# A graph and FFN kernel on one Trainium2 core: a ring of six one-tile one-hot units, one-hots made four (DVE) and five (ACT) slots ahead, and POOL's subtraction set behind the fold of position 35

## The chip, the cores and the metric

The kernel runs on one core of a Trainium2 chip. The metric is device time in microseconds (us) of one execution. The core has a matrix engine (PE, whose weight loads the profile lists as PEld), a vector engine (DVE), a scalar or activation engine (ACT), a general engine (POOL, also called GpSimd) and a queue for transfers (SP). Each runs its own instruction list strictly in order, and they meet at semaphores.

## The reference, cut to what matters

There are 8 batches of 1024 nodes with 128 channels. A graph layer takes for every node the elementwise maximum of its first 25 neighbours' normalised features, and an FFN with routed experts follows.

```python
x = x + gnn(adj, layernorm(x), W, b)
x = x + ffn(layernorm(x), route_id, Wi, bi, Wr, br, Ws, bs, Wo, bo)

def gnn(A, X, W, b):
    mask = A != 0
    scores = where(mask, -arange(N), -inf)
    vals, idx = top_k(scores, 25)
    feats = where(valid[..., None], X[idx], -inf)
    agg = feats.max(axis=2)
    agg = where(degree <= 25, maximum(agg, 0), agg)
    return relu(concat([X, agg]) @ W + b)
```

## The kernel before, in words

**The neighbour maximum as matmuls.** Nodes lie in eight tiles of 128. The first tile (the hub tile, with many neighbours) goes by a top-25 search on DVE and a gather of rows: POOL issues 25 indirect transfers a batch (`gather`, L508), the first 13 as one half and the last 12 as the other, two at a time (PACE is 2: the next pair waits until the last has landed). The other seven tiles of columns go through PE. For each source tile (or pair of tiles, group 5) and each rank r within it, the r-th neighbour of every node is picked by a one-hot matrix: PE multiplies the features of the source tile by it. Such a pair (group, rank) is a **slot**; there are NS = 44 slots to a batch, in the order of PLACES. Position p is the place of a slot in this order, and n = 44 * batch + p its number. A slot of full width has 7 tiles (896 columns, as 512 + 384); a narrow one has fewer. Positions 1, 13, 19, 20, 24 and 42 belong to the two-tile group 5 and have twice the matmuls and a one-hot of two tiles.

**The three steps of a slot.** (1) The one-hot is made in SBUF from `rank`: on DVE by one comparison (`tensor_scalar`, is_equal, L926) for the 16 positions of DVE_HOT (3, 5, 7, 13, 15, 16, 18, 19, 20, 23, 24, 31, 33, 36, 38, 42), on ACT for the 28 of ACT_HOT, by one activation (L636) where r is 1, otherwise by a square into `away` (`distance`, L625) and a second activation (L642). (2) PE runs the slot (`slot`, L730) into one of two PSUM buffers: it waits for the one-hot and for the fold of slot n - 2, which frees the buffer. (3) DVE folds the result into the running maximum `acc` (`fold_slot`, L937 for positions 0 and 1, L939 for the others), after PE has ended the slot.

**The ring before.** `onehot` has RING = 3 places of two tiles. ACT waits for slot n - 3 before it writes one-hot n. DVE needs no wait, as it writes one-hot n right behind its fold of slot n - 3 (AHEAD = 3).

**The order of the work.** All engines walk over (s, p), s from 0 to 9, p from 0 to 43. In stage s, batch s is prepared (masks, transposes, ranks, top-25), the slots of batch s - 1 are run, and the FFN of batch s - 2 (`finish`) is computed. So stages 1 to 8 hold slots, stage 9 holds only an FFN. What else is done at which position is written out by hand in tables. Those that matter here:

- ACT: at p = 7 the square root for the norms (L658), which waits for DVE's variance of the same position; at 9 and 11 four activations `h` each (L567); at 11, 13, 14, 16 the normalised `xn`; layer activations (L584) at 19 to 34; the ranks' evictions (L596) at 16, 18, 20, 22, 28, 32, 37, 38. ACT runs its one-hot for p + 3 and its square for p + 4 at the end of position p.
- DVE: variance at 7 and reciprocal root at 8 (small operations with drains between them); the search (`score`, `top`, L990, L998, L1000) at 11, 13, 17, 20, 21, 22, 25, 27; the gathered rows' maximum at 14 and 24 (first half) and 31 and 34 (second half). DVE's one-hot for p + 3 follows the fold of p.
- POOL: `split(b)` (L496) computes the low part of the features of batch b, `xsplit[:, b % 2, 1] = xn - xsplit[:, b % 2, 0]`, 1024 columns of float32. PE's slot 0 of the batch waits for it. Before, it is issued after the last gather of batch b - 1, in stage b.

Of the kernel before, what the change touches and what calls it, by code (L numbers as in the profile page):

```python
# [8 lines left out]
F32R = mybir.dt.float32r  # L9
# [6 lines left out]
P = 128  # L16
# [6 lines left out]
SPLITS = 3  # L23
PARTS = 2
CHUNKS = 2
AHEAD = 3
RING = 3
MASKS = 3
HALF = 13
PACE = 2  # L30
# [21 lines left out]
NS = len(SLOTS)  # L52
# [5 lines left out]
AWAYS = 2  # L58


def gnn_ffn_program(nc, x, adj, gnn_W, gnn_b, route_id, Wi, bi, Wr, br, Ws, bs, Wo, bo, out):
# [4 lines left out]
    COLS = TT * P  # L66
# [41 lines left out]
    W_AT = {14: [(0, 0)], 15: [(0, 1)], 16: [(1, 0)], 17: [(1, 1)]}  # L108
    LAYER_AT = [{19 + i: i for i in range(IT)}, {27 + i: i for i in range(IT)}]
    VERDICT_AT = 24  # L110
    FIRST_W_AT = 6
    OUT_AT = {36: 0, 39: 1}
    WEIGHTS_AT = [] + [NS + p for p in (
# [15 lines left out]
    with ExitStack() as ctx:  # L129
        def sb(name, shape, dt=F32):  # L130
            return ctx.enter_context(nc.sbuf_tensor(name, shape, dt))
# [41 lines left out]
        mask = sb("mask", [P, MASKS, N], BF16)  # L173
        at = sb("at", [P, IT, COLS], BF16)
        rank = sb("rank", [P, 2, IT, COLS], BF16)
        onehot = sb("onehot", [P, RING, 2, COLS], F32R)
        away = sb("away", [P, AWAYS, COLS], BF16)
        acc = sb("acc", [P, 2, COLS])
        aggT = sb("aggT", [P, COLS])
# [130 lines left out]
        def positions():  # L310

            for s in range(B + 2):
                for p in range(NS):
                    yield s, p

        def norms(s):

# [147 lines left out]
        @block.gpsimd  # L465
        def _(pool):
            pool.memset(ident[:, :], 0.0).then_inc(s_memset, 1)
            pool.memset(onesb[:, :], 1.0).then_inc(s_memset, 1)
            pool.wait_ge(s_memset, 2)
            pool.affine_select(out=ident[:, :], in_=ident[:, :], compare_op=ALU.not_equal, fill=1.0,  # L470
                               base=0, pattern=[[-1, P]], channel_multiplier=1).then_inc(s_memset, 1)

            pool.affine_select(out=before[:, :], in_=onesb[:, :], compare_op=ALU.is_gt, fill=0.0,
                               base=0, pattern=[[1, P]], channel_multiplier=-1).then_inc(s_memset, 1)
            pool.wait_ge(s_memset, 4)
            pool.affine_select(out=before[:, :], in_=before[:, :], compare_op=ALU.not_equal, fill=-float(NONE - 1),
                               base=0, pattern=[[1, P]], channel_multiplier=-1).then_inc(s_const, 1)
            pool.tensor_copy(identr[:, :], ident[:, :]).then_inc(s_const, 1)
            pool.iota(down[:, :], [[-1, N]], N, channel_multiplier=0,
                      allow_small_or_imprecise_dtypes=True).then_inc(s_const, 1)  # L480
            pool.iota(ranks[:, :], [[1, 32]], 1, channel_multiplier=0,
                      allow_small_or_imprecise_dtypes=True).then_inc(s_const, 1)
            pool.iota(base[:, :], [[1, 1]], N, channel_multiplier=0,
                      allow_small_or_imprecise_dtypes=True).then_inc(s_const, 1)
            pool.iota(lane[:, :], [[1, 1]], 0, channel_multiplier=1,
                      allow_small_or_imprecise_dtypes=True).then_inc(s_const, 1)
            pool.memset(gath[:, HALF:HALF + B, :], 0.0).then_inc(s_const, 1)
            pool.wait_ge(s_const, CONSTS)
            for q in range(4):
                pool.wait_ge(s_adj[q], 16)  # L490
            for b in range(B):
                pool.dma_start(tables[b][N:TABROW, :], gath[:, HALF + b, :]).then_inc(s_zero, 16)
            def split(b):

                pool.wait_ge(s_hi, b + 1)
                pool.tensor_tensor(xsplit[:, b % 2, 1], xn[:, :, :], xsplit[:, b % 2, 0].bitcast(F32),  # L496
                                   ALU.subtract).then_inc(s_split, 1)

            def gather(b, h, entries, signal, reduced):

                pool.wait_ge(s_idx, b * HUBS + h + 1)
                if b + h > 0:
                    pool.wait_ge(reduced, b * HUBS + h)
                pool.wait_ge(s_tab[b % 2], 16 * (b // 2 + 1))
                for i, j in enumerate(entries):
                    if i > 0 and i % PACE == 0:
                        pool.wait_ge(signal, 16 * (len(entries) * (b * HUBS + h) + i))
                    pool.indirect_dma_start(gath[:, j, :], None, tables[b],  # L508
                                            bass.IndirectOffsetOnAxis(ap=idx[:, b % 2, h, j:j + 1], axis=0)
                                            ).then_inc(signal, 16)  # L510

            split(0)
            for m in range(NIN):
                pool.dma_start(w_in[m], raw_weight(m)).then_inc(s_wfirst[m // 4], 16)
            for n, (g, t, cap) in enumerate(CAP_RUNS):
                if t == 0:
                    pool.memset(caps[:, g:g + 1], float(cap)).then_inc(s_caps, 1)
                else:
                    pool.wait_ge(s_caps, n)
                    pool.affine_select(out=caps[:, g:g + 1], in_=caps[:, g:g + 1], compare_op=ALU.is_gt,  # L520
                                       fill=float(cap), base=t * B, pattern=[[-1, 1]], channel_multiplier=-1
                                       ).then_inc(s_caps, 1)
            pool.wait_ge(s_zero, 16 * B)
            for b in range(B):
                for h in range(HUBS):
                    gather(b, h, range(HALF), s_gathA, s_redA)
                    gather(b, h, range(HALF, TOPK), s_gathB, s_redB)
                if b + 1 < B:
                    split(b + 1)

            def tile_again(t, b, one, dma):
                pool.wait_ge(s_const, CONSTS)
                pool.wait_ge(r_idx, one)
                for j in range(TOPK):
                    pool.indirect_dma_start(gath[:, j, :], None, tables[b],
                                            bass.IndirectOffsetOnAxis(ap=idx[:, 0, 0, j:j + 1], axis=0)
                                            ).then_inc(r_gath, 16)
            again(pool, tile_again)

        @block.scalar  # L540
        def _(act):
# [86 lines left out]
            def one_hot(n):  # L628
                b, p = divmod(n, NS)
                g, r, wide = SLOTS[p]  # L630
                first, many = GROUPS[g]
                if n >= RING:
                    act.wait_ge(s_slot, n - RING + 1)
                if r == 1:
                    act.wait_ge(s_q, 2 * IT * b + 2 * (first + many))
                    act.activation(onehot[:, n % RING, 0:many, 0:wide * P],  # L636
                                   rank[:, b % 2, first:first + many, 0:wide * P],
                                   ACT.Relu, bias=ranks[:, 1:2], scale=-1.0).then_inc(s_acthot, 1)
                else:
                    i = b * len(SQUARED) + SQUARED.index(p)  # L640
                    act.wait_ge(s_away, i + 1)
                    act.activation(onehot[:, n % RING, 0, 0:wide * P], away[:, i % AWAYS, 0:wide * P],  # L642
                                   ACT.Relu, bias=1.0, scale=-1.0).then_inc(s_acthot, 1)

            for s, p in positions():
# [17 lines left out]
                if s < B and p in MASK_AT[s > 0]:  # L663
# [3 lines left out]
                    if n >= MASKS:  # L667
                        act.wait_ge(s_turn[n % MASKS], 16 * (n // MASKS))
                    act.activation(mask[:, n % MASKS, :], adj_sb[:, q % 4, :].bitcast(U32), ACT.Sign  # L669
                                   ).then_inc(s_mask, 1)  # L670
                for ahead, body, slots in ((AHEAD, one_hot, ACT_HOT), (AHEAD + 1, distance, SQUARED)):
                    n = (s - 1) * NS + p + ahead
                    if 0 <= n < B * NS and n % NS in slots:
                        body(n)
# [32 lines left out]
        def _(pe):  # L707
# [6 lines left out]
            def slot(b, p):  # L714
# [11 lines left out]
                for j in range(many):  # L726
                    for part in range(PARTS):
                        for c0 in range(0, wide * P, BANK):
                            c1 = min(c0 + BANK, wide * P)
                            mm = pe.matmul(slot_ps[n % 2][:, c0:c1], xsplit[:, b % 2, part, first + j, :],  # L730
                                           onehot[:, n % RING, j, c0:c1], start=(j == 0 and part == 0),
                                           stop=(j == many - 1 and part == PARTS - 1))
                mm.then_inc(s_slot, 1)

# [171 lines left out]
        def _(dve):  # L906
# [13 lines left out]
            def one_hot(n):  # L920
# [2 lines left out]
                first, many = GROUPS[g]  # L923
                if p == min(q for q in DVE_HOT if SLOTS[q][0] == g):
                    dve.wait_ge(s_q, 2 * IT * b + 2 * (first + many))
                dve.tensor_scalar(onehot[:, n % RING, 0:many, 0:wide * P],  # L926
                                  rank[:, b % 2, first:first + many, 0:wide * P], ranks[:, r - 1:r], None,
                                  ALU.is_equal).then_inc(s_onehot, 1)

# [221 lines left out]
            for s, p in positions():  # L1151
                if 1 <= s <= B:
                    fold_slot(s - 1, p)
                ahead = (s - 1) * NS + p + AHEAD
                if 0 <= ahead < B * NS and ahead % NS in DVE_HOT:
                    one_hot(ahead)
                if 1 <= s <= B and p == NS - 1:
# [85 lines left out]
```

## Time and profile before

| | us |
|---|---|
| median of 3 runs (747.49 to 750.78) | 750.15 |
| the profiled execution's own time | 748.9 |
| its span, first to last instruction | 747.2 |
| PE, DVE, ACT, POOL busy in it | 610.9, 615.6, 567.8, 238.2 |
| matmuls of the slots (L730), 1376 | 371.2 |
| folds (L939), 336 | 292.6 |
| stage 1, from the first matmul of its slot 0 | 106 |
| stages 2 to 7 | 79 to 81 each |
| stage 8 | 75 |
| stage 9 | 47 |

All times of instructions come from the profiled execution and are us from the start of its span. The granted clock of PE is given as a share of full speed: 1.00 is 2.4 GHz and 0.50 is 1.2 GHz. A busy share over the whole run says little here, because each stage passes through stretches with different limits. So the stages are cut into stretches of four positions, at the starts of DVE's folds (the folds are the L937 and L939 instructions, 44 to a stage, in order).

### The profile page before, as it was taken

What the parts mean: (1) busy time and instruction counts of PE and PEld (TensorE: products, weight loads), DVE (VectorE), ACT (ScalarE), POOL (GpSimd) and SP (SyncE); (2) the same over time, 40 slices, a digit from 0 to 9 for tenths busy, and PEclk for the clock granted to TensorE, in tenths of its full rate; (3) what the DMA queues carried; (4) which work ended last, traced back from release to release, by engine and by line L of the source; (5) the groups of instructions that cost most, each with busy time, mean ns of one, the idle gap of its engine ahead of it and who ended that gap; (6) DMA issues with size and microseconds to landing.
All of it is one profiled execution on the core that took longest, in us unless ns stands there. A gap on an engine that the chain in (4) does not pass through costs nothing.

```text
span 747.2 us, 11820 instructions
## 1 busy us (share of the span) xinstructions
PE 610.9 (82%) x3496; PEld 501.5 (67%) x3497; DVE 615.6 (82%) x1047; ACT 567.8 (76%) x1053; POOL 238.2 (32%) x260
## 2 busy tenths in 40 slices
PE   0464766769997899969996999788996999799786
PEld 0053644557886688847985788667875888589665
DVE  3775898889998899879998999889987998778740
ACT  5664554679897988889897889797988997678262
POOL 4522225433543324333243413332434234410000
PEclk9997898989999799979997999889997999799989
DMA  9999995399647855695549755874566463135222
GB/s 303 308 191 287 303 349 187 124 236 299 183 134 197 227 146 140 148 254 170 158 110 224 224 142 146 197 226 126 142 156 161 122 165 93 29 84 155 57 70 77
DMA packets 145171, 131.73 MB, mean 176 GB/s; under 512 B 72219, under 2 KB 112324, under 8 KB 145092
## 3 DMA queue, kind: packets, MB, share of 16 engines
q1 hardware_dynamic: 128124, 105.94, 53.0%
q0 software_dynamic: 7296, 15.74, 8.2%
q10 hardware_dynamic: 9680, 9.21, 4.3%
q8 instruction: 31, 0.51, 0.3%
q14 instruction: 40, 0.33, 0.1%
HBM read 98.20 MB, written 17.98 MB: 155 GB/s over the span
## 4 chain that ended last, share of the span: by engine, by line
PE 51%; DVE 26%; issue 8%; ACT 5%; DMA 5%; DVEq 2%; SPq 2%; ACTq 0%
PE slot_ps L730 24%; PE ffn_ps L795 10%; DVE acc L939 9%; DVE onehot L926 5%; PE ffn_ps L805 4%; DMA at<-mask 3%; DVE score L1000 3%; DVE top L998 2%; PE prep_ps L822 2%; DMA adj_sb<-in_adj_dram 2%; PE ffn_ps L745 2%; SPq L393 2%; PE ffn_ps L779 2%; PE ffn_ps L764 2%; DVE wst L1104 1%
## 5 line engine op out<-in xcount | busy, mean ns | idle before, releaser
L730 PE MATMUL slot_ps<-onehot,xsplit 128*128 128x512 f32 (+3 forms) x1376 | 371.2, 399 | 61.8 <-ACT onehot L642 32.9
L939 DVE TENSOR_TENSOR acc<-slot_ps,acc 128x896 f32<-128x896 f32 (+2 forms) x336 | 292.6, 882 | 52.2 <-PE slot_ps L730 45.9
L730 PEld LDWEIGHTS slot_ps<-onehot,xsplit 128*128 128x128 f32 x1376 | 251.0, 204 | 118.3 <-issue 52.4
L508 POOL DMA_INDIRECT gath<-feature_table,idx x200 | 202.4, 1012 | 400.2 <-DMA gath<-feature_table,idx 294.8
L642 ACT ACTIVATE onehot<-away 128x896 fp32r<-128x896 bf16 (+3 forms) x168 | 118.6, 706 | 23.7 <-PE slot_ps L730 10.0
L795 PE MATMUL ffn_ps<-hT,wst 128*128 128x128 f32 x1024 | 135.2, 277 | 0.0
L625 ACT ACTIVATE away<-rank,ranks 128x896 bf16<-128x896 bf16 (+3 forms) x168 | 132.9, 791 | 0.6 <-DVE wst L1104 0.6
L795 PEld LDWEIGHTS ffn_ps<-hT,wst 128*128 128x128 f32 x1024 | 129.0, 191 | 5.7 <-issue 0.6
L926 DVE TENSOR_SCALAR onehot<-rank,ranks 128x896 fp32r<-128x896 bf16 (+3 forms) x128 | 106.7, 834 | 0.0
L584 ACT ACTIVATE hT<-ffn_ps,wst 128x128 f32<-128x128 f32 x256 | 81.1, 374 | 33.4 <-PE ffn_ps L795 31.7
L596 ACT ACTIVATE rank<-prep_ps 128x448 bf16<-128x448 f32 x128 | 62.9, 549 | 24.4 <-PE prep_ps L822 12.9
L669 ACT ACTIVATE mask<-adj_sb 128x1024 bf16<-128x1024 uint32 x56 | 58.7, 1047 | 22.4 <-DMA at<-mask 19.4
L636 ACT ACTIVATE onehot<-rank,ranks 128x896 fp32r<-128x896 bf16 (+1 forms) x56 | 64.5, 1152 | 10.9 <-PE slot_ps L730 10.2
L822 PE MATMUL prep_ps<-at,before 128*128 128x448 bf16 x128 | 40.2, 384 | 14.8 <-DMA at<-mask 12.0
L861 PE MATMUL ffn_ps<-ident,hT 128*128 128x128 f32 x136 | 23.8, 303 | 32.3 <-DVE wst L1104 28.8
L861 PEld LDWEIGHTS ffn_ps<-ident,hT 128*128 128x128 f32 x136 | 17.1, 155 | 41.5 <-issue 40.2
L998 DVE MAX8 top<-score 128x8 f32<-128x1024 f32 x32 | 39.0, 1217 | 0.3
L779 PE MATMUL ffn_ps<-xnT,wiT 128*128 128x512 f32 x64 | 33.7, 615 | 0.0
L805 PE MATMUL ffn_ps<-woT,hT 128*128 128x128 f32 x256 | 32.8, 281 | 0.0
L805 PEld LDWEIGHTS ffn_ps<-woT,hT 128*128 128x128 f32 x256 | 29.8, 191 | 3.6 <-issue 3.6
L822 PEld LDWEIGHTS prep_ps<-at,before 128*128 128x128 bf16 x128 | 11.4, 99 | 30.6 <-DMA at<-mask 12.1
L1000 DVE MATCH_REPLACE8 score<-top,score 128x1024 f32<-128x1024 f32 x24 | 29.0, 1206 | 0.0
(120 smaller groups left out, 528.8 us busy)
## 6 DMA issues: line engine op xcount, KB each, us to landing
wst<-folded_weights SPq DMA_DIRECT2D x128, 257.0 KB
adj_sb<-in_adj_dram SPq DMA_DIRECT2D x64, 512.0 KB
folded_weights<-wst ACTq DMA_DIRECT2D x34, 256.0 KB
hT<-in_L_ffn_Wr_dram SPq DMA_DIRECT2D x26, 256.0 KB
xs<-in_x_dram SPq DMA_DIRECT2D x8, 512.0 KB
feature_table<-xn SPq DMA_DIRECT2D x8, 512.0 KB
x<-in_x_dram SPq DMA_DIRECT2D x8, 512.0 KB
out_dram<-h SPq DMA_DIRECT2D x16, 256.0 KB, 2.7
```

The lines of the kernel that those rows point to most:

```text
L508: pool.indirect_dma_start(gath[:, j, :], None, tables[b], bass.IndirectOffsetOnAxis(ap=idx[:, b % 2, h, j:j + 1], axis=0)).then_inc(signal ...
L584: ins = act.activation(hT[:, 1 - l, j, i, :], ffn_ps[(i + 1) % 2][:, j * P:(j + 1) * P], ACT.Relu, bias=wst[:, i, HC * HID + j:HC * HID + ...
L596: act.activation(rank[:, s % 2, jt, c * CW:(c + 1) * CW], prep_f[c][:, 0:CW], ACT.Copy, bias=float(NONE)).then_inc(s_q, 1)
L625: act.activation(away[:, i % AWAYS, 0:wide * P], rank[:, b % 2, first, 0:wide * P], ACT.Square, bias=ranks[:, r - 1:r], scale=-1.0).then_i ...
L636: act.activation(onehot[:, n % RING, 0:many, 0:wide * P], rank[:, b % 2, first:first + many, 0:wide * P], ACT.Relu, bias=ranks[:, 1:2], sc ...
L642: act.activation(onehot[:, n % RING, 0, 0:wide * P], away[:, i % AWAYS, 0:wide * P], ACT.Relu, bias=1.0, scale=-1.0).then_inc(s_acthot, 1)
L730: mm = pe.matmul(slot_ps[n % 2][:, c0:c1], xsplit[:, b % 2, part, first + j, :], onehot[:, n % RING, j, c0:c1], start=(j == 0 and part == ...
L795: mm = pe.matmul(ffn_ps[(i + 1) % 2][:, j * P:(j + 1) * P], wst[:, i, c0:c0 + P], hT[:, l, kc, i, :], start=(kc == 0), stop=(kc == HC - 1))
L805: mm = pe.matmul(o, hT[:, 0, kc, i, :], woT[:, kc, :], start=False, stop=(i % 4 == 3 and kc == HC - 1))
L822: mm = pe.matmul(prep_f[c][:, 0:CW], before[:, :], at[:, jt, cols], start=True, stop=not second)
L926: dve.tensor_scalar(onehot[:, n % RING, 0:many, 0:wide * P], rank[:, b % 2, first:first + many, 0:wide * P], ranks[:, r - 1:r], None, ALU. ...
L939: dve.tensor_tensor(acc[:, p % 2, 0:cols], slot_ps[n % 2][:, 0:cols], acc[:, p % 2, 0:cols], ALU.max).then_inc(s_max, 1)
```

## The change

The ring becomes six units of one tile each (the same memory). A slot of one tile takes one unit, a two-tile slot takes two that lie side by side, from unit 0 again where they don't fit. `FREE[n]` is the number of slots that PE must have ended before one-hot n may be written. ACT makes its one-hots five positions ahead (squares six), DVE four. DVE waits for the ring only where its own folds don't already imply it (that is at one position of batch 0). ACT waits by FREE. Worked out by the function `ring`, a one-hot of ACT waits for slot n - 6 at positions 8 to 12 and 30 to 41, for slot n - 4 at positions 21 and 22 of every batch and at 25, 26 and 27 of every other, for slot n - 3 or n - 4 at positions 1 and 2, and mostly for slot n - 5 elsewhere.

POOL's `split(b)` for b > 0 leaves its place behind the gathers of batch b - 1. It is issued within the first half of the gathers of batch b, after the first four, and waits until DVE has folded position 35 of stage b.

```diff
-AHEAD = 3
-RING = 3
+ACT_AHEAD = 5
+DVE_AHEAD = 4
+UNITS = 6
+    SPLIT_AFTER, SPLIT_BATCH = 35, 4
-        onehot = sb("onehot", [P, RING, 2, COLS], F32R)
+        onehot = sb("onehot", [P, UNITS, COLS], F32R)
+        def ring():
+
+            unit, free, last = [], [], [0] * UNITS
+            u = 0
+            for n in range(B * NS):
+                many = GROUPS[SLOTS[n % NS][0]][1]
+                if u + many > UNITS:
+                    u = 0
+                unit.append(u)
+                free.append(max(last[u:u + many]))
+                for i in range(u, u + many):
+                    last[i] = n + 1
+                u = (u + many) % UNITS
+            return unit, free
+
+        UNIT, FREE = ring()
...
                 for i, j in enumerate(entries):
+                    if entries[0] == 0 and i == SPLIT_BATCH and b > 0:
+                        pool.wait_ge(s_max, (b - 1) * NS + SPLIT_AFTER + 1)
+                        split(b)
                     if i > 0 and i % PACE == 0:
...
                     gather(b, h, range(HALF, TOPK), s_gathB, s_redB)
-                if b + 1 < B:
-                    split(b + 1)
...
-                if n >= RING:
-                    act.wait_ge(s_slot, n - RING + 1)
+                if FREE[n] > 0:
+                    act.wait_ge(s_slot, FREE[n])
-                    act.activation(onehot[:, n % RING, 0:many, 0:wide * P],
+                    act.activation(onehot[:, UNIT[n]:UNIT[n] + many, 0:wide * P],
...
-                for ahead, body, slots in ((AHEAD, one_hot, ACT_HOT), (AHEAD + 1, distance, SQUARED)):
+                for ahead, body, slots in ((ACT_AHEAD, one_hot, ACT_HOT), (ACT_AHEAD + 1, distance, SQUARED)):
...
-                                           onehot[:, n % RING, j, c0:c1], start=(j == 0 and part == 0),
+                                           onehot[:, UNIT[n] + j, c0:c1], start=(j == 0 and part == 0),
...
-                dve.tensor_scalar(onehot[:, n % RING, 0:many, 0:wide * P],
+                if FREE[n] > max(0, n - DVE_AHEAD + 1):
+                    dve.wait_ge(s_slot, FREE[n])
+                dve.tensor_scalar(onehot[:, UNIT[n]:UNIT[n] + many, 0:wide * P],
...
-                ahead = (s - 1) * NS + p + AHEAD
+                ahead = (s - 1) * NS + p + DVE_AHEAD
```

## Rows read from the trace of the kernel before

**Rows 1.** Windows, stage 5: span, busy (x count) of PE, PEld, DVE, ACT, POOL, clock, DMA, GB/s
```profile
384.20:464.80 80.60, 72.59 (x419) 61.00 (x420) 72.42 (x118) 69.81 (x132) 26.84 (x26) 0.94 0.65 175
```

**Rows 2.** Waits of PE in stages 2 to 7 (145 to 625 us): total, times, longest
```profile
PE slot_ps L730 <- ACT onehot L642: 26.1, 10, 3.5
PE slot_ps L730 <- DVE acc L939: 18.5, 33, 2.1
```

**Rows 3.** Windows, positions 20 to 24 of stages 2 to 7, columns as in rows 1
```profile
184.22:191.49 7.27, 7.27 (x54) 6.72 (x54) 7.19 (x11) 5.99 (x15) 2.02 (x2) 1.00 0.91 279
263.99:273.34 9.35, 8.08 (x58) 7.31 (x57) 9.24 (x12) 7.83 (x20) 4.57 (x3) 1.00 0.49 131
344.34:353.12 8.78, 8.06 (x58) 7.29 (x57) 8.68 (x11) 7.47 (x18) 4.26 (x3) 1.00 0.51 136
424.18:433.53 9.35, 8.05 (x58) 7.30 (x57) 9.25 (x11) 7.83 (x20) 4.63 (x3) 1.00 0.51 131
504.70:514.84 10.14, 8.03 (x58) 7.27 (x56) 10.06 (x12) 7.33 (x18) 4.27 (x3) 1.00 0.54 144
586.08:594.10 8.02, 8.02 (x58) 7.31 (x57) 8.02 (x12) 6.71 (x18) 1.31 (x1) 1.00 0.48 131
```

**Rows 4.** Windows, positions 28 to 32 of stages 2 and 3
```profile
199.16:207.37 8.21, 7.02 (x51) 6.46 (x49) 8.04 (x13) 6.01 (x14) 4.20 (x4) 1.00 0.56 155
281.00:287.35 6.35, 6.35 (x47) 6.04 (x46) 6.17 (x14) 5.87 (x13) 1.91 (x3) 1.00 0.64 159
```

**Rows 5.** Timeline: one-hot of position 24 in stage 1; subtraction and the same one-hot, stage 5
```profile
98.12 0.74 DVE L926 TENSOR_SCALAR onehot<-rank,ranks 128x1024 fp32r<-128x1024 bf16 x1
...
427.15 2.39 POOL L496 TENSOR_TENSOR xsplit<-xn,xsplit 128x1024 fp32r<-128x1024 f32 x1
427.30 2.80 DVE L926 TENSOR_SCALAR onehot<-rank,ranks 128x1024 fp32r<-128x1024 bf16 x1
```

**Rows 6.** Windows, positions 8 to 12 and 12 to 16 of stage 5
```profile
400.85:408.33 7.48, 3.39 (x10) 2.93 (x11) 6.14 (x14) 7.27 (x14) 2.87 (x4) 0.65 0.72 171
...
408.33:417.67 9.34, 9.34 (x33) 7.06 (x32) 7.01 (x11) 8.20 (x18) 2.80 (x3) 0.73 1.03 305
```

**Rows 7.** Timelines of DVE, ACT and PE, stage 5, positions 7 to 12: start, us, instruction
```profile
400.85 1.08 DVE L939 TENSOR_TENSOR acc<-slot_ps,acc 128x896 f32<-128x896 f32 x1
403.42 0.54 DVE L939 TENSOR_TENSOR acc<-slot_ps,acc 128x384 f32<-128x384 f32 x1
404.93 1.09 DVE L939 TENSOR_TENSOR acc<-slot_ps,acc 128x896 f32<-128x896 f32 x1 [0.96 <-PE slot_ps L730]
405.93 1.15 DVE L926 TENSOR_SCALAR onehot<-rank,ranks 128x1792 fp32r<-128x1792 bf16 x1
...
400.97 0.22 ACT L658 ACTIVATE std<-mv 128x16 f32<-128x16 f32 x1 [2.75 <-DVE mv L964]
...
403.02 2.18 PE L730 MATMUL slot_ps<-onehot,xsplit 128*128 128x512 f32 x6 [3.25 <-ACT onehot L642]
407.13 1.01 PE L730 MATMUL slot_ps<-onehot,xsplit 128*128 128x384 f32 x2 [1.92 <-ACT onehot L642]
```

**Rows 8.** Timeline, stage 1: POOL's fourth gather of batch 1, DVE's one-hot 42
```profile
136.57 0.95 POOL L508 DMA_INDIRECT gath<-feature_table,idx  x1 [0.31 <-issue]
...
139.80 1.14 DVE L926 TENSOR_SCALAR onehot<-rank,ranks 128x1792 fp32r<-128x1792 bf16 x1
```

**Rows 9.** Timelines, stage 5: POOL's last gather, DVE's use of it, fifth gather, fold 35, one-hot 42
```profile
426.18 0.95 POOL L508 DMA_INDIRECT gath<-feature_table,idx  x1 [0.30 <-issue]
...
446.88 0.95 DVE L1036 TENSOR_TENSOR gath<-gath 128x768 f32<-128x768 f32 x1
...
452.55 0.95 POOL L508 DMA_INDIRECT gath<-feature_table,idx  x1 [2.52 <-DMA gath<-feature_table,idx]
...
453.53 1.08 DVE L939 TENSOR_TENSOR acc<-slot_ps,acc 128x896 f32<-128x896 f32 x1
...
459.93 1.14 DVE L926 TENSOR_SCALAR onehot<-rank,ranks 128x1792 fp32r<-128x1792 bf16 x1
```

More of the change, by code:

```diff
@@ L641, in one_hot @@
                     act.wait_ge(s_away, i + 1)
-                    act.activation(onehot[:, n % RING, 0, 0:wide * P], away[:, i % AWAYS, 0:wide * P],
+                    act.activation(onehot[:, UNIT[n], 0:wide * P], away[:, i % AWAYS, 0:wide * P],
                                    ACT.Relu, bias=1.0, scale=-1.0).then_inc(s_acthot, 1)
```

## The prediction

> **What bounds the kernel now.** I first cut the trace into stages. Stages 2 to 7 are alike; in stage 5 PE is busy for 72.6 and DVE for 72.4 of 80.6 us [rows 1]. Neither alone explains the length, so the two must take turns at being last. The list of waits says whom PE waits for in these six stages: 26.1 us in all for ACT's one-hots, in only ten long waits, and 18.5 us for DVE's folds, in 33 short ones [rows 2]. A total of this kind overstates what can be won, because a wait is put down to the last of several releasers. So I cut each stage into stretches of four positions, at the starts of the folds, and read where the six stages differ and where all engines but one have idle time.
>
> Two stretches stand out. Positions 20 to 24 take 7.27 us in stage 2 and 8.02 to 10.14 us in stages 3 to 7, with DVE busy for practically all of the time in each [rows 3]. Stage 2 pays the same surplus later: positions 28 to 32 take 8.21 us there and 6.35 in stage 3 [rows 4]. The timeline names the cause. The one-hot of position 24 takes 0.74 us on DVE when it is alone, and 2.80 us in stage 5, where POOL's subtraction began 0.15 us before it and lasted 2.39 us [rows 5]. DVE's instruction ends 0.56 us behind POOL's: it stood still while POOL worked.
>
> The second stretch is positions 8 to 12: PE is busy for only 3.39 of 7.48 us, and in the next four positions it is the limit, at 9.34 of 9.34 us, with a mean granted clock of 0.73, that is partly at 1.2 GHz [rows 6]. Here PE waits for ACT twice: 3.25 us up to slot 10 and 1.92 us up to slot 12. ACT is late because it makes one-hot 10 behind the square root of position 7, for which it waited 2.75 us on DVE [rows 7].
>
> **The change, part by part**, against the profiled execution's 748.9 us.
>
> *The subtraction leaves DVE's one-hots.* Against stage 2's 7.27 us, stages 3 to 7 lose 2.08, 1.51, 2.08, 2.87 and 0.75 us, 9.3 together [rows 3]; stage 2 loses 8.21 - 6.35 = 1.86 [rows 4]. Sum 11.1 us. The other end is that PE's own work sets these stretches as soon as DVE is quicker: PE is busy there for 8.08, 8.06, 8.05, 8.03 and 8.02 us, which leaves 5.4 us, and 8.21 - 7.02 = 1.2 in stage 2; together 6.6. I take 11.1, since stage 2 is the same code without the collision, and the four matmuls that the others have more [rows 3] are PE running ahead into the next slot. **-11.1**, bounds -6.6 and -11.1.
>
> *The subtraction at its new place.* Fold 35 of stage 5 ends at 454.6. POOL then works until 457.0. DVE's next one-hot will be that of position 42, now made behind fold 38 rather than 39; it begins at 459.9 now [rows 9] and would begin some 1.0 us earlier, at 458.9, 1.9 us clear of POOL. Between them DVE runs only folds, statistics and the output's addition. One case is worse: in stage 1 the fourth gather ends at 137.5, later than fold 35, so the subtraction runs from 137.5 to 139.9. One-hot 42 begins at 139.80 there today [rows 8]; one full fold (1.1 us) earlier it begins at 138.7 and stands until 139.9: **+1.2**, bounds 0 and the whole 2.4.
>
> The page "SBUF — State Buffer" of the Trainium skill, in its section "Who interferes with whom", calls this an exclusive lock between GpSimd and a DVE instruction in a two-port mode, tensor_scalar among them: whoever begins first blocks the other fully. The trace agrees, by the 2.80 us [rows 5]. The page also lets a DVE instruction with two SBUF inputs collide with a GpSimd instruction that reads SBUF. By that rule the gathered rows' maximum could be blocked as well when it falls on the subtraction; at most one such case, in stage 1, would add the subtraction's 2.4 us once, and the sum would be 2.4 us higher.
>
> *What else POOL's queue holds.* The 5th and later gathers of a batch stand behind the new wait. In stage 5 the fifth would go out at 457.0 instead of 452.55, 4.5 us later. The last gather of a batch goes out at 426.18 and DVE first needs it at 446.88 [rows 9]: 20.7 us less 0.95 us and its landing. Cover is ample: 0. If it were gone, the cost would be the excess over it, on DVE at position 31. PE's slot 0 needs the subtraction eight positions later, more than 10 us: 0.
>
> *ACT further ahead.* One-hots 10 and 11 come before the square root of position 7, in ACT's 2.75 us of waiting, and one-hot 12 right behind it. Slot 10 can then start when fold 8 ends, at 401.93, instead of 403.02: 1.09 us [rows 7]. Slot 12 needs the end of fold 10. DVE now makes one-hot 13 (two tiles, 1.15 us) behind fold 9, which ends at 403.96, and so in front of fold 10: fold 10 again ends at about 406.0. Slot 12 starts there instead of at 407.13: 1.1 us. This, and not the sum of both waits, is what the stage gains, for from slot 12 on PE is the limit [rows 6]. **-1.1** for each of six stages and -0.5 for stage 8, whose load is lighter: **-7.1**. Bounds: 0, if DVE is late for another reason, and -2.2 a stage, -13.7.
>
> *PE's clock.* PE idles 2.1 and some 1.6 us instead of 3.25 and 1.92, and its work from slot 12 on is gapless 1.1 us earlier, so it may return to 2.4 GHz sooner. If it never fell, positions 12 to 16 would be set by DVE, busy for 7.01 of 9.34 us: -2.3 a stage [rows 6]. The other end is nothing. Two long pauses remain, so I take a value near nothing, -0.3 for six stages: **-1.8**.
>
> *DVE's one-hots one position earlier.* The same work lands elsewhere: positions 8 to 12 get 0.7 us more, 4 to 8 and 28 to 32 as much less. **0**, bounds -2.5 and +2.5.
>
> *ACT's ring.* At positions 21, 22 and (every other batch) 25 to 27, ACT waits for the slot after the one it is at, with the FFN's layer activations queued behind. PE needs such an activation two positions later: **0** as long as that holds; the slower rival below prices the failure. Stage 9 and the start have no such one-hots: 0.
>
> Sum: 748.9 - 11.1 + 1.2 - 7.1 - 1.8 = 730.1 us. The profiled execution is 1.25 us under the median of the three runs, so half of that is added: **731**.
>
> **The rivals.**
>
> *PE's clock holds.* The lead closes enough of the pauses, and PE stays at 2.4 GHz through positions 8 to 16. For it: the clock is 1.00 wherever PE has no long pause [rows 3, 4]. Against it: 2.1 us of pause before slot 10 remain, as fold 8 isn't made earlier. Two more us in six stages: 719. The page "TensorE: Matmul & The Clock Gate", Part 1, has the same rule: the clock is throttled by default and activity releases it; by it too the result hangs on how much PE does in this stretch.
>
> *The lead gives nothing.* The folds between 400.85 and 406.02 are a chain on DVE of its own, and one-hot 13 within it takes what ACT's earlier one-hots give. Only the subtraction pays: 748.9 - 11.1 + 1.2 = 739.0, with the same half us 740. For it: DVE is busy for 6.14 of 7.48 us there, and drains lie between the small operations.
>
> *The subtraction isn't clear of the one-hots.* If folds 36 to 38 pass faster than I think, or POOL starts late, it meets one-hot 42 in each stage, and up to 1.9 us come back in six stages: 731 + 11.4, some 742.
>
> *Slower: ACT is held by the ring.* The place is positions 21 to 27. Each of 2 to 5 tight waits a batch would hold a layer activation for one slot of PE, about 1.05 us, and PE, which has no wait for them now, would stand for it: 3.5 x 1.05 x 7 = 26 us on top of 739, 765. The cost begins at the point where ACT's layer activation is over two positions late. Against it: ACT has 1.3 to 2.8 us idle in positions 20 to 24 of stages 2 to 7, [rows 3].
>
> **How the numbers follow.** The forecast (731) gets 0.57, the clock 0.10, no gain from the lead 0.19, the lost clearance 0.09, slower 0.05. A measurement of this kernel can tell about 0.5% from no change, 3.75 us, here 746.4 to 753.9. All cases but the last lie under 746.4, and of the lost clearance a part could reach it: faster 0.92, same 0.04, slower 0.04. For the range, the bounds of the forecast's terms give 731 - 7 (lead and one-hots) and 731 + 9 (the subtraction's lesser bound and part of the lead); it is opened to 721 and 742, which leaves out the slower case and half of the clock's.
>
> **What would show it right or wrong.** Right: no one-hot of DVE over 1.3 us in stages 2 to 7; positions 20 to 24 near 7.3 us in all of these; the wait before slot 10 about 2.1 us instead of 3.25 and released by DVE; ACT's one-hots no releaser of PE to speak of; stages of about 77 us. Wrong: a one-hot 42 over 2 us on DVE, layer matmuls (L795) that wait for ACT, a maximum of gathered rows that waits for transfers, or stretches that stay at their old length with DVE idle.

## The result and the profile after

The changed kernel takes 737.27 us (median of 4 runs, 735.39 to 739.00) against 748.82 for the kernel before in the same measurements: a ratio of 0.985, with a 95% interval of 0.980 to 0.989. The forecast was 731 us with a range of 721 to 742. The direction and the range held, but only three fifths of the expected gain came: 11.5 us instead of 19.

The profiled execution took 739.0 us, with a span of 737.3. The first lines of its page:

```profile
span 737.3 us, 11826 instructions
## 1 busy us (share of the span) xinstructions
PE 612.4 (83%) x3496; PEld 500.2 (68%) x3497; DVE 605.3 (82%) x1047; ACT 567.5 (77%) x1053; POOL 238.0 (32%) x260
```

DVE is busy for 10.3 us less than before (605.3 against 615.6). PE isn't: the gain is idle time, and time in which DVE stood still. PE's list of waits for the whole run, after, shows whose it was.

```profile
PE slot_ps L750 <- DVE acc L961: 42.5, 54, 2.3
PE ffn_ps L881 <- DVE wst L1126: 31.3, 20, 7.1
PE slot_ps L750 <- ACT onehot L662: 3.0, 2, 2.7
```

ACT's one-hots have left the list, but for two waits (2.67 us for slot 0 of stage 1, 0.37 at 61.7 us). In stages 2 to 7 they had 26.1 us [rows 2]. In their place PE waits for DVE's folds (L961 is the old L939).

**Positions 20 to 24**, stages 2 to 7, after, in windows with the columns of rows 1, answer to [rows 3].

```profile
186.69:193.53 6.84, 6.84 (x50) 6.28 (x49) 6.59 (x11) 6.21 (x14) 2.90 (x4) 1.00 0.82 261
264.48:271.27 6.79, 6.79 (x49) 6.23 (x49) 6.58 (x10) 6.21 (x14) 3.04 (x4) 1.00 0.49 137
342.57:349.36 6.79, 6.79 (x49) 6.23 (x49) 6.58 (x10) 6.20 (x14) 2.84 (x3) 1.00 0.54 144
420.65:427.44 6.79, 6.79 (x49) 6.23 (x49) 6.59 (x10) 6.20 (x14) 3.35 (x4) 1.00 0.55 141
497.76:504.56 6.80, 6.80 (x49) 6.24 (x49) 6.59 (x11) 6.29 (x15) 3.00 (x3) 1.00 0.52 136
575.79:582.58 6.79, 6.79 (x49) 6.23 (x49) 6.58 (x11) 6.21 (x14) 1.90 (x2) 1.00 0.52 141
```

All six stages are alike now, where they took 7.27 to 10.14 us before. PE is busy for all of it. The last half microsecond, from 7.27 to 6.79, is no gain by itself: the cuts lie at folds, and a one-hot that DVE makes one fold earlier can move across a cut. One-hot 23 has left these positions, and one-hot 31 has come into 24 to 28, which take 8.28 us now in stages 3, 4, 6 and 7 and took 7.66 before.

**Positions 8 to 12 and 12 to 16**, stage 5, after, answer to [rows 6], and the timelines of DVE and PE to [rows 7].

```profile
398.29:405.33 7.04, 4.19 (x13) 0.57 1.02 241
...
405.33:414.61 9.28, 9.28 (x33) 0.77 1.04 314
```

```profile
398.29 1.08 DVE L961 TENSOR_TENSOR acc<-slot_ps,acc 128x896 f32<-128x896 f32 x1
401.23 1.26 DVE L948 TENSOR_SCALAR onehot<-rank,ranks 128x1792 fp32r<-128x1792 bf16 x1
402.41 1.27 DVE L961 TENSOR_TENSOR acc<-slot_ps,acc 128x896 f32<-128x896 f32 x2
...
399.52 2.59 PE L750 MATMUL slot_ps<-onehot,xsplit 128*128 128x512 f32 x6 [2.31 <-DVE acc L961]
403.63 0.98 PE L750 MATMUL slot_ps<-onehot,xsplit 128*128 128x384 f32 x2 [1.52 <-DVE acc L961]
```

The windows are of PE alone here: span, PE busy, clock, DMA, GB/s. Slot 10 starts 0.15 us behind the end of fold 8, as foretold, after a pause of 2.31 us instead of 3.25. Slot 12 starts behind fold 10, in front of which one-hot 13 now stands, as foretold too. Yet 8 to 12 shrank by only 0.44 us, 12 to 16 by 0.06. Counted from the start of fold 8, slot 12 starts 0.94 us earlier than before and fold 13 begins 0.96 earlier, but fold 16 only 0.50: from fold 13 on DVE has no pause, and it now makes the two-tile one-hot 19 (1.15 us) in front of fold 16 instead of behind it.

**Where the time went.** Cut at the first fold of each stage, one profile each, in us:

| kernel | ratio to before (95%) | stage 1 | stages 2 to 7 | stage 8 |
|---|---|---|---|---|
| before | 1 | 104.4 | 480.1 | 72.7 |
| changed | 0.985 (0.980 to 0.989) | 107.7 | 466.7 | 73.3 |
| split_only | 0.994 (0.991 to 0.998) | 110.7 | 469.6 | 72.9 |
| leads_only | 0.995 (0.992 to 0.999) | 108.4 | 472.4 | 73.1 |
| dve_lead_3 | 0.980 (0.976 to 0.985) | 112.7 | 458.1 | 71.4 |
| stage1_split_old | 0.985 (0.980 to 0.990) | 104.7 | 465.8 | 72.9 |
| lead3_stage1_old | 0.970 (0.965 to 0.974) | 106.7 | 458.3 | 71.3 |
| act_lead_4 | 0.969 (0.964 to 0.973) | 106.7 | 457.1 | 72.1 |
| dve4_act3 | 0.992 (0.989 to 0.995) | 109.8 | 472.4 | 73.0 |
| onehot13_late | 0.978 (0.974 to 0.982) | 107.6 | 464.3 | 71.9 |
| late_two_back | 0.985 (0.982 to 0.988) | 109.5 | 464.6 | 73.6 |

The changed kernel gains 13.4 us in stages 2 to 7 and loses 3.3 in stage 1 and 0.5 in stage 8. How far one profile can be trusted shows in two pairs that run the same code in stages 2 to 7: changed and stage1_split_old differ there by 0.9 us, dve_lead_3 and lead3_stage1_old by 0.2. A difference of about 1 us in this column isn't shown.

The same six stages by positions, mean of a stage in us:

| kernel | 0 to 8 | 8 to 16 | 16 to 24 | 24 to 36 | 36 to 44 |
|---|---|---|---|---|---|
| before | 14.6 | 16.6 | 15.3 | 22.1 | 11.4 |
| split_only | 14.6 | 16.6 | 13.8 | 21.8 | 11.5 |
| changed | 14.1 | 16.1 | 12.9 | 22.0 | 12.6 |
| dve_lead_3 | 14.6 | 14.5 | 13.9 | 21.9 | 11.5 |
| onehot13_late | 14.1 | 15.0 | 13.6 | 22.0 | 12.6 |

### The profile page after: what moved, and what is told of

The parts are those of the page before. It is cut to its first block, busy times and chain, and to the rows that moved or that the text cites. A ratio compares the mean times of both kernels' runs of the same rounds, so it can differ in the third digit from the quotient of the medians.

```text
span 737.3 us, 11826 instructions
## 1 busy us (share of the span) xinstructions
PE 612.4 (83%) x3496; PEld 500.2 (68%) x3497; DVE 605.3 (82%) x1047; ACT 567.5 (77%) x1053; POOL 238.0 (32%) x260
## 4 chain that ended last, share of the span: by engine, by line
PE 61%; DVE 21%; DMA 5%; issue 5%; ACT 4%; SPq 2%; DVEq 2%; ACTq 0%
PE slot_ps L750 29%; PE ffn_ps L815 15%; DVE acc L961 9%; PE prep_ps L842 3%; DMA at<-mask 3%; PE ffn_ps L799 3%; PE ffn_ps L825 2%; DMA adj_sb<-in_adj_dram 2%; PE ffn_ps L784 2%; DVE onehot L948 2%; PE ffn_ps L765 2%; DVE gath L1039 2%; DVE wst L1126 1%; PE ffn_ps L785 1%; DVE stats L1142 1%
## 5 line engine op out<-in xcount | busy, mean ns | idle before, releaser
L961 DVE TENSOR_TENSOR acc<-slot_ps,acc 128x896 f32<-128x896 f32 (+2 forms) x336 | 293.9, 883 | 51.6 <-PE slot_ps L750 49.4
L662 ACT ACTIVATE onehot<-away 128x896 fp32r<-128x896 bf16 (+3 forms) x168 | 118.7, 707 | 21.7 <-PE slot_ps L750 10.3
L948 DVE TENSOR_SCALAR onehot<-rank,ranks 128x896 fp32r<-128x896 bf16 (+3 forms) x128 | 94.8, 741 | 2.4 <-PE slot_ps L750 2.4
L656 ACT ACTIVATE onehot<-rank,ranks 128x896 fp32r<-128x896 bf16 (+1 forms) x56 | 66.0, 1179 | 11.4 <-PE slot_ps L750 10.7
L842 PEld LDWEIGHTS prep_ps<-at,before 128*128 128x128 bf16 x128 | 11.4, 99 | 32.1 <-DMA at<-mask 11.7
L515 POOL TENSOR_TENSOR xsplit<-xn,xsplit 128x1024 fp32r<-128x1024 f32 x8 | 19.2, 2400 | 38.7 <-DVE acc L961 31.2
```

Source lines behind the costliest of these rows:

```text
L656: act.activation(onehot[:, UNIT[n]:UNIT[n] + many, 0:wide * P], rank[:, b % 2, first:first + many, 0:wide * P], ACT.Relu, bias=ranks[:, 1: ...
L662: act.activation(onehot[:, UNIT[n], 0:wide * P], away[:, i % AWAYS, 0:wide * P], ACT.Relu, bias=1.0, scale=-1.0).then_inc(s_acthot, 1)
L842: mm = pe.matmul(prep_f[c][:, 0:CW], before[:, :], at[:, jt, cols], start=True, stop=not second)
L948: dve.tensor_scalar(onehot[:, UNIT[n]:UNIT[n] + many, 0:wide * P], rank[:, b % 2, first:first + many, 0:wide * P], ranks[:, r - 1:r], None ...
L961: dve.tensor_tensor(acc[:, p % 2, 0:cols], slot_ps[n % 2][:, 0:cols], acc[:, p % 2, 0:cols], ALU.max).then_inc(s_max, 1)
```

## The experiments

**The subtraction's move alone.**

```diff
 # on the kernel before: AHEAD = 3, RING = 3 stay
+                    if entries[0] == 0 and i == 4 and b > 0:
+                        pool.wait_ge(s_max, (b - 1) * NS + 36)
+                        split(b)
...
-                if b + 1 < B:
-                    split(b + 1)
```

> The kernel before (ring of three, lead 3) with nothing but POOL's subtraction moved behind the fold of position 35. Theory A (the subtraction's place is most of the gain, and is worth the 11.1 us of the prediction): stages 2 to 7 lose 11 us together, positions 20 to 24 take 7.3 us in each, and the time is 0.985 of the kernel before, near 738. In stage 1 the subtraction begins about 137.5, behind DVE's reduction of the gathered rows, so nothing is lost there. Theory B (PE's own work fills the stretches as soon as DVE is quicker): only the lower bound of 6.6 us comes, 0.991, near 742.

Median 745.58 us, ratio 0.994. Theory A is right on stages 2 to 7 and wrong on stage 1, where it expected no loss. Stages 2 to 7 lose 10.5 us, and positions 20 to 24 fall to stage 2's 7.27 in stages 3 to 7; three of them, with the columns of rows 1:

```profile
268.56:275.86 7.30, 7.30 (x54) 6.74 (x54) 7.20 (x11) 5.99 (x15) 3.29 (x4) 1.00 0.56 160
347.00:354.27 7.27, 7.27 (x54) 6.72 (x54) 7.19 (x11) 5.98 (x15) 2.72 (x3) 1.00 0.65 168
...
582.46:589.73 7.27, 7.27 (x54) 6.72 (x54) 7.19 (x11) 5.98 (x15) 2.00 (x2) 1.00 0.61 158
```

But stage 1 took 6.3 us more. Its timeline, DVE, POOL and PE:

```profile
136.65 3.08 DVE L1018 TENSOR_TENSOR half_max<-gath,half_max 128x128 f32<-128x128 f32 x1
140.02 0.69 DVE L1105 TENSOR_TENSOR wst<-ffn_ps,x 128x512 f32<-128x512 f32 x1
...
136.25 0.94 POOL L511 DMA_INDIRECT gath<-feature_table,idx  x1 [0.30 <-issue]
137.21 2.36 POOL L496 TENSOR_TENSOR xsplit<-xn,xsplit 128x1024 fp32r<-128x1024 f32 x1
...
140.85 1.08 PE L862 MATMUL ffn_ps<-ident,hT 128*128 128x128 f32 x4 [4.92 <-DVE wst L1105]
```

The subtraction doesn't meet a one-hot there. It meets a maximum over gathered rows, which takes 0.29 us alone and 3.08 here. The folding of weights behind it is late, and PE, which transposes the next weights, waits for 4.92 us (1.86 at this place before). Then the clock falls: it is at half from 139.83 to 150.07, where the kernel before keeps full clock. Positions 36 to 40 of stage 1, before and with the move alone (columns as in rows 1; the clock is the third number from the end):

```profile
131.36:141.46 10.10, 6.42 (x36) 4.64 (x36) 9.75 (x19) 6.53 (x10) 4.50 (x5) 1.00 0.41 133
```

```profile
130.90:146.14 15.24, 8.38 (x36) 6.12 (x36) 12.68 (x19) 6.63 (x10) 9.43 (x9) 0.79 0.33 101
```

The same 36 matmuls take 8.38 us instead of 6.42. The stretch is 5.1 us longer. Of this the hold is 2.8 (3.08 less 0.29). Another 1.1 isn't the subtraction's: DVE waited 1.08 us for a gather to land, up to 132.38, and this gather's pair had been issued 3.5 us later than before, in a part in which both kernels run the same code. The rest, 1.3, and 1.5 more in positions 40 to 44, fall where PE runs at half its clock. The changed kernel has the hold without that wait, and its stage 1 is 3.3 us longer than before:

```profile
134.55 3.90 DVE L1039 TENSOR_TENSOR gath<-gath 128x384 f32<-128x384 f32 x3
...
135.94 2.35 POOL L515 TENSOR_TENSOR xsplit<-xn,xsplit 128x1024 fp32r<-128x1024 f32 x1
...
139.94 1.09 PE L881 MATMUL ffn_ps<-ident,hT 128*128 128x128 f32 x4 [4.50 <-DVE wst L1126]
```

The row of DVE joins three maxima; the last of them began at 135.53 and took 2.92 us instead of 0.29.

**The leads alone.**

```diff
 # on the changed kernel
-                    if entries[0] == 0 and i == SPLIT_BATCH and b > 0:
-                        pool.wait_ge(s_max, (b - 1) * NS + SPLIT_AFTER + 1)
-                        split(b)
...
+                if b + 1 < B:
+                    split(b + 1)
```

> The changed kernel (ring of six, ACT five and DVE four ahead) with POOL's subtraction back behind the gathers of the batch before. Theory A (the longer leads are worth little: what ACT's lead gives, DVE's earlier one-hots take): time within 4 us under the kernel before, 0.994 to 1.000, and positions 20 to 24 long again. Theory B (the leads are worth the 7 us and more of the prediction, and something else in the changed kernel costs them): 0.988 or less, near 740.

Median 744.95 us, ratio 0.995, inside theory A's figure, but only as stage 1 is 4.0 us longer than before: stages 2 to 7 are 7.7 us shorter. And positions 20 to 24 weren't long again, but for stage 7. DVE makes one-hot 24 in position 20, and the subtraction came in position 21, when DVE ran the search, so in stages 3, 4 and 6 it met nothing. In stages 2 and 5 it met the maximum over gathered rows, in stage 7 one-hot 24 (2.66 us), and in stage 1 a one-hot (3.30 us). Stage 2 in the timelines of POOL and DVE, and positions 24 to 28 of stages 2 and 3:

```profile
197.13 2.95 DVE L1038 TENSOR_TENSOR half_max<-gath 128x128 f32<-128x128 f32 x1
...
197.54 2.38 POOL L515 TENSOR_TENSOR xsplit<-xn,xsplit 128x1024 fp32r<-128x1024 f32 x1
```

```profile
195.17:206.10 10.93, 8.96 (x62) 7.87 (x60) 10.61 (x12) 8.79 (x21) 4.29 (x3) 1.00 0.49 135
275.38:283.66 8.28, 8.18 (x59) 7.42 (x58) 7.96 (x12) 8.14 (x20) 0.00 (x0) 1.00 0.58 162
```

So the two halves of the change share a part of their gain: a different order of DVE's one-hots takes half of the collisions away by itself. In stages 2 to 7 the move is worth 10.5 us alone and 5.7 on top of the leads; the leads are worth 7.7 alone and 2.9 on top of the move.

**DVE's lead back at three.**

```diff
-DVE_AHEAD = 4
+DVE_AHEAD = 3
```

> The changed kernel with DVE's one-hots three slots ahead again, ACT's still five. Theory A (one-hot 13 stands in front of fold 10, and one-hots 42 and 3 in front of late folds, so that DVE's lead of four costs what ACT's lead gives): slot 12 starts about 1.1 us earlier behind fold 10, stages 2 to 7 are about 76.8 us instead of 77.8, and the time is 5 to 8 us under the changed kernel, near 731. Theory B (DVE's order doesn't matter, its folds and PE take turns anyway): within 2 us of the changed kernel.

Ratio 0.980. Stages 2 to 7 are 8.6 us shorter than with a lead of four, where theory A had six. The total doesn't show it: the median is 734.62 against 737.27, and the intervals of the ratios overlap. Stage 5, positions 8 to 12 (columns as in rows 1):

```profile
398.77:405.10 6.33, 4.49 (x14) 3.48 (x15) 5.96 (x14) 5.83 (x11) 2.88 (x3) 0.61 0.89 250
```

Fold 10 now ends 4.0 us behind the start of fold 8 instead of 5.2, and slot 12 starts right behind it. DVE (fold 9 and fold 10 in one row, then one-hot 13) and PE:

```profile
401.18 1.61 DVE L961 TENSOR_TENSOR acc<-slot_ps,acc 128x384 f32<-128x384 f32 x2
402.71 1.14 DVE L948 TENSOR_SCALAR onehot<-rank,ranks 128x1792 fp32r<-128x1792 bf16 x1
...
402.94 0.98 PE L750 MATMUL slot_ps<-onehot,xsplit 128*128 128x384 f32 x2 [0.40 <-DVE acc L961]
```

Stage 1 is the longest of all at 112.7 us, 5 us over the changed kernel's, which hides that much of the gain in the total. Of the 5 us 3.8 lie in positions 8 to 12, where DVE waited 9.86 us for the transfer of the adjacency (`adj_sb`), against 5.46 in the changed kernel.

**The subtraction for batch 1 at its old place.**

```diff
-                    if entries[0] == 0 and i == SPLIT_BATCH and b > 0:
+                    if entries[0] == 0 and i == SPLIT_BATCH and b > 1:
...
+                if b == 0:
+                    split(1)
```

> The changed kernel, but the subtraction for batch 1 keeps its old place in front of batch 1's gathers; those of batches 2 to 7 stay behind fold 35. Theory A (in stage 1 the subtraction stops DVE's maximum over gathered rows for 2.4 us, and DVE is the limit there): stage 1 is 2.4 to 3.3 us shorter, the whole near 734.5. Theory B (stage 1 waits for loads and for the folding of weights anyway): same time within 1 us.

Stage 1 fell by 3.0 us, to 104.7, and the maximum over gathered rows takes its usual time again. The medians (735.99 against 737.27) and ratios don't separate the two kernels: the intervals are wider than the effect.

**Both together, and a smaller lead of ACT.** The second has `ACT_AHEAD = 4` besides.

> The changed kernel with DVE's lead back at three and the subtraction for batch 1 at its old place. Theory A (three effects that hardly touch each other: collisions, ACT's lead, DVE's lead): stages 2 to 7 stay at 458 us as with DVE's lead of three alone, stage 1 goes from 112.7 to about 104.5, the whole is 8 us under dve_lead_3, 725 to 727, faster than both kernels. Theory B (stage 1's length is set by its loads and varies by itself): stage 1 stays over 110 and the time is that of dve_lead_3, 734.

> As lead3_stage1_old, with ACT four positions ahead instead of five. Theory A (what counts is that one-hot 10 comes ahead of the square root of position 7, which a lead of four does): time within 2 us of lead3_stage1_old, though one-hot 12 is made in position 8 only. Theory B (the full lead is needed because ACT is busy all through positions 8 to 20): 3 us or more slower, with PE waiting for ACT's one-hot at position 12 or 17.

Ratios 0.970 and 0.969, medians 728.50 and 727.39 us: both beat both kernels, and they can't be told apart. The first is a little above its 725 to 727. Against dve_lead_3 its stage 1 is 6 us shorter, though 106.7 and not 104.5. Only 3.0 of these lie in positions 36 to 40, where the collision was; 2.1 lie in positions 8 to 12, where DVE waits for the adjacency, and aren't the subtraction's. So the old place is worth about 3 us in both comparisons, and the 1% between the two ratios overstates it. ACT's lead of four is enough, so theory B for it falls: PE waits no more for ACT's one-hots (L664) than with five. PE's waits over the whole run, lead3_stage1_old first:

```profile
PE slot_ps L752 <- DVE acc L963: 34.7, 49, 2.3
PE ffn_ps L883 <- DVE wst L1128: 29.2, 19, 8.0
...
PE slot_ps L752 <- ACT onehot L664: 3.0, 2, 2.7
```

```profile
PE slot_ps L752 <- DVE acc L963: 33.7, 46, 2.3
PE ffn_ps L883 <- DVE wst L1128: 27.2, 17, 8.3
...
PE slot_ps L752 <- ACT onehot L664: 2.7, 1, 2.7
```

**DVE's lead of four without ACT's.**

```diff
-ACT_AHEAD = 5
+ACT_AHEAD = 3
```

> The changed kernel with ACT's lead back at three, DVE's at four: the cost of DVE's lead of four without ACT's gain. Theory A (DVE's earlier one-hots cost by themselves, whatever ACT does): slower than split_only, stages 2 to 7 some 3 to 8 us longer together than its 469.6. Theory B (DVE's lead costs only where ACT's lead has made DVE the limit): the same as split_only within 2 us, 745.

Ratio 0.992. Stages 2 to 7 took 472.4 us, 2.8 more than split_only's 469.6, just under theory A's 3 to 8. In total it can't be told from split_only (0.994). So DVE's lead costs 2.8 us while ACT is late anyway, and 8.6 once ACT isn't: its price is mostly gain that it takes from the other. Read the other way, ACT's lead gives 11.5 us with DVE's at three and 5.7 with DVE's at four. The ring of six units is in all of these but split_only; no run has it with both leads at three, so its own part isn't told apart from ACT's lead.

**Which of DVE's one-hots?** First one-hot 13 alone three ahead, as below, then one-hots 42 and 3 alone, with `in (3, 42)` in place of `== 13`:

```diff
-                ahead = (s - 1) * NS + p + DVE_AHEAD
-                if 0 <= ahead < B * NS and ahead % NS in DVE_HOT:
-                    one_hot(ahead)
+                for lead in (3, 4):
+                    ahead = (s - 1) * NS + p + lead
+                    if 0 <= ahead < B * NS and ahead % NS in DVE_HOT and lead == (3 if ahead % NS == 13 else 4):
+                        one_hot(ahead)
```

> The changed kernel with one edit: DVE makes one-hot 13 (two tiles) three ahead, behind fold 10, all its others four ahead. Theory A (one-hot 13 in front of fold 10 is most of the cost of DVE's lead): positions 8 to 16 shrink from 16.2 to about 14.5 us in each of stages 2 to 7, which are 8 to 10 us shorter together; the time is near 729. Theory B (the late positions, 36 to 44, carry the cost): 2 us or less from 737.

> The changed kernel with two of DVE's one-hots three ahead again: that of position 42 (two tiles, behind fold 39) and that of position 3 (behind fold 0 and the merge of the batch before); one-hot 13 and the rest stay four ahead. Theory A (these two stand in front of folds that PE waits for, as one-hot 13 does): positions 36 to 44 shrink from 12.6 to 11.4 us in stages 2 to 7, their 466.7 us become about 460, and the time is near 731. Theory B (the extra time in positions 24 to 44 is PE's backlog, moved there from earlier positions): the stretch shrinks but another grows, and the time stays within 2 us of the changed kernel.

Both of my theories A missed in size. One-hot 13 is worth 2.4 us in stages 2 to 7 (464.3 against 466.7), not 8 to 10. Stage 2 is spoilt in this profile: PE waited 2.20 us there for the transfer of a mask (up to 182.37). Stages 3 to 7 show 3.8 us. Positions 8 to 16 did shrink, from 16.1 to 15.0 us and not to 14.5, but 16 to 24 grew from 12.9 to 13.6. The ratio (0.978) agrees with dve_lead_3's within their intervals, so the total alone would have flattered the theory.

One-hots 42 and 3 are worth 2.1 us in stages 2 to 7, but 1.1 in stages 3 to 7, which is little more than two runs of the same code differ by. In total (0.985) this kernel can't be told from the changed one, so theory B stands. Positions 40 to 44 shrink from 6.4 to 5.7 us, and positions 0 to 4 grow from 6.7 to 7.2. That needn't be a backlog: one-hot 3 is now made in positions 0 to 4, and DVE is busy for 0.6 us more in them.

No single one-hot carries the 8.6 us. In stages 3 to 7 the changed kernel and dve_lead_3 differ by 6.9 us, of which 4.0 are idle time of PE (time less busy time, by windows of these stages) and 2.9 are PE's matmuls taking longer. The clock doesn't explain the 2.9: split_only has dve_lead_3's busy time of PE (356.8 us) with 51.2 us at half the clock, against 37.5. Of the 6.9, one-hot 13 is 3.8, and one-hots 42 and 3 about 1.1. What makes up the rest stays open.

## Why the prediction was right or wrong

The forecast's sum took 18.8 us off the profiled execution; it fell by 9.9, from a span of 747.2 to 737.3. In stages 2 to 7 19.5 us were foretold and 13.4 came, in stage 1 a loss of 1.2 and it was 3.3, in stage 8 a gain of 0.5 and it was a loss of 0.5. So the time lies in the range, but of the terms that weren't nought only the first came out near its figure.

- **The subtraction leaves DVE's one-hots, -11.1.** Right: -10.5 in stages 2 to 7, by the move alone. Stage 2 had been a fair measure of a stage without the collision, and PE's busy time no floor.
- **The subtraction at its new place, +1.2.** The mechanism was missed in the sum. In stages 2 to 7 the new place is clear, as foretold: no one-hot of DVE is over 1.3 us. In stage 1 the sum priced a collision with one-hot 42. What was hit was a maximum over gathered rows, at positions 36 and 37 in this stage, and stage 1 was 3.3 us longer in the changed kernel and 6.3 with the move alone (1.1 of these a gather's landing). I had the instruction's length right (2.4 us) but took that for the price. The price also held a late fold of weights, PE's wait for it and a fallen clock. The Trainium skill, in "SBUF — State Buffer", section "Who interferes with whom", named this: a DVE instruction with two SBUF inputs and a GpSimd instruction that reads SBUF exclude each other. The trace agrees (3.08 us for 0.29); the sentence on it in the prediction stood beside the sum, and its 2.4 us were nearer than the sum's 1.2.
- **ACT further ahead, -7.1 with one-hot 13 netted in, and the clock, -1.8.** ACT's lead, with the ring of six, is the difference of dve_lead_3 and split_only: 11.5 us in stages 2 to 7. The chain was right: slot 10 behind fold 8, slot 12 behind fold 10, and positions 8 to 16 fell by 2.1 us a stage, near the bound of 2.2 without one-hot 13. For six stages that bound and the clock's term were 15.0 us, so 3.5 are missing here. The netting wasn't enough either.
- **DVE's one-hots one position earlier, 0 with bounds of 2.5.** This is the step that failed, by its mechanism and not by its size alone. Its full price is 8.6 us in stages 2 to 7, of which the prediction had 6.6 within the term for one-hot 13. In stages 3 to 7 alone the price is 6.9: one-hot 13 is 3.8 of it, where 5.5 were foretold, and the others are 3.1, where 0 was. That is more than the bound of 2.5 that the term had for all six. The two errors partly cancel, so the price came out only 1.4 us off in these five stages, which is luck. I had counted the same work at another place as nothing, stretch by stretch. DVE's fold is what frees PE's buffer, so each instruction put in front of a fold delays PE wherever PE waits for it: in stages 2 to 7 PE waits 33.5 us for folds in the changed kernel and 25.8 in dve_lead_3. Net of everything, the leads gave 2.9 us in stages 2 to 7 on top of the move, where 8.4 were foretold: 3.5 us of the difference are on the side of ACT and the clock, 2.0 on DVE's.
- **The clock.** The granted clock still fell around positions 8 to 12 in each stage (0.57 in the window above, 0.65 before [rows 6]). The rival in which it holds is refuted. PE's busy time in these positions rose from 3.39 to 4.19 us (13 matmuls instead of 10), and the clock fell all the same. It came back sooner in stages 6 and 7, after 6.8 us at half instead of 10.2, and as late as before in stages 3 to 5. That this paid isn't shown: against stages 3 to 5 stage 6 is 0.9 us shorter, stage 7 only 0.2. The rule of the Trainium skill ("TensorE: Matmul & The Clock Gate", Part 1), that activity releases the throttle, isn't contradicted: in stage 5 PE was back at full clock at 409.57, within positions 12 to 16, having worked without a pause since 403.63.
- **The rival "the lead gives nothing", 740**, comes nearest in time, and half of its cause is right. ACT's lead gave 11.5 us, and DVE's earlier one-hots took 8.6 of them back. But one-hot 13, which the rival names, was only a part of that, 2.9 us were left, and the losses in stages 1 and 8 did the rest. That it came so near is partly luck.
- **The lost clearance, 742.** It didn't occur: in stages 2 to 7 one-hot 42 takes its usual time. It is the second nearest in time, by luck.
- **The slower rival** didn't occur. In stages 2 to 7 PE never waits for ACT's layer activations in the changed kernel.
- **Gathers behind the new wait, 0.** Right: the last gather of a batch went out at 431.3 us in stage 5, in position 25, and PE or DVE didn't wait for any.

## What to carry to other kernels

Where an instruction of one engine can hold up one of another (here POOL's subtraction and DVE, 3.08 us for 0.29), list for every place where a long instruction could go what the other engine does there in each stage, the odd first stage included, and every form that can be blocked. Look-ahead is worth having on the engine that is late (ACT here, by 11.5 us) and can cost on the engine whose next instruction frees the consumer's buffer (DVE here, by 8.6); change them apart. And a wait removed from the longest chain is worth what stands right behind it, which a run with one part undone shows better than the sum.

## What the runs showed that I had not expected

DVE's instruction was held before the subtraction's record begins. With the move alone the maximum began at 136.65, while POOL was issuing a gather (136.25 to 137.19), and the subtraction at 137.21. DVE's instruction ended at 139.73, so it stood through both. A gather's issue alone does little in these traces: it lengthens a one-hot of DVE by some 0.2 us at most, and a maximum over gathered rows, 0.29 us, to 0.37 at most. The long hold comes when the subtraction follows directly.

It can also be POOL that stands. With DVE's lead at three, one-hot 38 comes right behind fold 35, for which POOL's subtraction waits. In stage 5 of dve_lead_3 the one-hot began 0.17 us before the subtraction and took its usual 0.68 us, and the subtraction took 2.77 us instead of 2.39, as does that of every stage from 2 to 7:

```profile
448.31 2.77 POOL L515 TENSOR_TENSOR xsplit<-xn,xsplit 128x1024 fp32r<-128x1024 f32 x1 [4.76 <-DVE acc L961]
...
448.14 0.68 DVE L948 TENSOR_SCALAR onehot<-rank,ranks 128x896 fp32r<-128x896 bf16 x1
```

Here POOL had been idle for 4.76 us, and not issuing a gather. Who stands can't be read off the starts of the two records, as the prediction's rule ("whoever begins first blocks the other fully") would have it: the held maximum above had begun first too. What decides it stays open.

A stage's length can be a poor guide to one execution: stage 1, which waits for loads and for weights to be folded, took between 104.4 and 112.7 us in these kernels, with DVE busy for 88 to 91 us of it. One wait for a transfer in it differed by 4.4 us between two kernels (9.86 against 5.46). So a difference of a few us in the length of stage 1 shows nothing by one profile each, until it is found in the stretch where its cause lies.
